# Attention a's outputs: halves and transposes moved from the tail into the head slots

## The reference

```python
x = x + _L0_attn_a_ref(_layernorm(x), Wq, Wk, Wv, bq, bk, bv, Wo, bo)   # 16 heads, softmax(q k^T / 8) v, then out @ Wo + bo
x = x + _L0_ffn_ref(_layernorm(x), w1, b1, w2, b2)                      # relu(x w1 + b1) w2 + b2, width 512
x = x + _L0_attn_b_ref(_layernorm(x), W_qk, W_v, alibi_slope)           # causal, scores + (kpos - qpos) * slope
x = x + _L0_ffn_ref(_layernorm(x), w1, b1, w2, b2)
return x
```

## Time and profile before

| | us |
|---|---|
| three runs | 563.72, 560.90, 563.49 |
| median | 563.49 |
| span of the profiled execution | 561.3 |
| PE busy | 526.3 (94%) |
| DVE busy | 446.3 (80%) |
| ACT busy | 469.0 (84%) |
| POOL busy | 453.8 (81%) |

### The profile page before, as it was taken

How to read it: one execution, slowest core, us unless ns; L and a number is a source line. 1 busy time by engine, 2 the same in 40 slices (tenths; PEclk the granted TensorE clock), 3 DMA queues, 4 the chain that set the end, 5 groups by cost and what they waited for, 6 DMA issues and landing times.

```text
span 561.3 us, 17932 instructions
## 1 busy us (share of the span) xinstructions
PE 526.3 (94%) x6864; PEld 371.1 (66%) x6864; DVE 446.3 (80%) x1382; ACT 469.0 (84%) x925; POOL 453.8 (81%) x447
## 2 busy tenths in 40 slices
PE   4888999999999999999999999998989998798897
PEld 3654666666666666766667666675679695656576
DVE  5878888888888888888888888887785575788943
ACT  3888998999988999989999899998973978573995
POOL 5678989888888888888888888888983977654885
PEclk9979999999999999999999999999999999998999
DMA  9442343332433324333243332435147100000002
GB/s 227 109 113 57 72 110 86 96 96 68 114 87 97 95 64 118 87 95 96 60 122 80 102 97 58 124 78 198 40 151 272 68 3 2 1 1 2 1 21 57
DMA packets 35461, 48.03 MB, mean 86 GB/s; under 512 B 10777, under 2 KB 16817, under 8 KB 35377
## 3 DMA queue, kind: packets, MB, share of 16 engines
q1 hardware_dynamic: 33264, 46.35, 30.2%
q10 hardware_dynamic: 2112, 0.54, 0.4%
HBM read 12.27 MB, written 9.44 MB: 39 GB/s over the span
## 4 chain that ended last, share of the span: by engine, by line
PE 75%; DVE 8%; issue 6%; ACT 5%; POOL 5%; DMA 1%; DVEq 0%; POOLq 0%; ACTq 0%
PE psum L562 11%; PE psum L620 10%; PE psum L621 10%; PE psum L516 7%; PE psum L518 6%; PE psum L517 6%; PE psum L600 6%; PE psum L602 6%; PE psum L601 6%; PE psum L623 2%; POOL h_lo L2146 1%; PE psum L781 1%; POOL rstd L2024 1%; ACT xn L1164 1%; DVE st_lo L1515 1%
## 5 line engine op out<-in xcount | busy, mean ns | idle before, releaser
L2079 POOL TENSOR_TENSOR p_hl<-p,p_hl 128x512 f16<-128x512 f32 x288 | 328.5, 1165 | 48.4 <-ACT p_hl L1264 44.6
L1532 DVE CUSTOM_DVE_ANT_0 max_junk<-psum,mask_s 128x1024 bf16<-128x1024 f32 (+7 forms) x256 | 190.4, 753 | 32.7 <-issue 32.6
L1263 ACT ACTIVATE p<-psum 128x512 f32<-128x512 f32 x288 | 175.9, 611 | 13.8 <-PE psum L623 12.2
L1264 ACT ACTIVATE p_hl<-psum 128x512 f16<-128x512 f32 x288 | 177.2, 615 | 0.0
L620 PE MATMUL psum<-q_hl,k_hh 128*128 128x512 f16 (+3 forms) x384 | 125.6, 327 | 0.5 <-ACT p_hl L1264 0.4
L600 PE MATMUL psum<-v_all,p_hl 128*128 128x65 f16 x1152 | 124.8, 193 | 1.1 <-POOL p_hl L2079 1.0
L601 PE MATMUL psum<-v_all,p_hl 128*128 128x64 f16 x1152 | 124.9, 192 | 0.0
L602 PE MATMUL psum<-v_all,p_hl 128*128 128x65 f16 x1152 | 124.4, 194 | 0.0
L621 PE MATMUL psum<-q_hm,k_l 128*128 128x512 f16 (+3 forms) x384 | 122.3, 327 | 0.0
L600 PEld LDWEIGHTS psum<-v_all,p_hl 128*128 128x128 f16 x1152 | 107.1, 98 | 16.1 <-POOL p_hl L2079 1.2
L601 PEld LDWEIGHTS psum<-v_all,p_hl 128*128 128x128 f16 x1152 | 106.2, 97 | 4.8
(11 more groups left out here) (206 smaller groups left out, 1109.1 us busy)
## 6 DMA issues: line engine op xcount, KB each, us to landing
k_hh<-st_hi SPq DMA_DIRECT2D x64, 128.0 KB, 2.3
o_scratch<-o_sb SPq DMA_DIRECT2D x16, 512.0 KB, 2.6
o_in<-o_scratch SPq DMA_DIRECT2D x8, 1024.0 KB, 8.6
q_hl<-st_hi SPq DMA_DIRECT2D x32, 128.0 KB, 2.4
q_hl<-st_lo SPq DMA_DIRECT2D x32, 128.0 KB, 2.4
k_l<-st_lo SPq DMA_DIRECT2D x32, 128.0 KB, 2.3
q_hm<-st_hi SPq DMA_DIRECT2D x32, 128.0 KB, 2.4
x_sb<-in_L_attn_a_x SPq DMA_DIRECT2D x4, 256.0 KB, 3.9
```

The source lines that it names most:

```text
L1263: nc.scalar.activation(p32[:, ring_at(u, r), :], src, ACT.Exp, scale=SCALE_A).then_inc(exp_done, 1)
L1264: nc.scalar.activation(p_hl[:, u % 2, 0, BANK * r:BANK * (r + 1)], src, ACT.Exp, scale=SCALE_A).then_inc(phi_done, 1)
L1532: nc.vector.tensor_tensor_reduce(out=max_junk[:, n % 2, 0:cols], in0=max_banks(v, j, 0, cols), in1=mask_s[:, S - cols:S], scale=1.0, scala ...
L2079: nc.gpsimd.tensor_tensor(p_hl[:, u % 2, 1, cols], p32[:, ring_at(u, r), :], p_hl[:, u % 2, 0, cols], ALU.subtract)\
```

## The change

The transposes of attention a's output no longer run on PE in the tail.

1. In slot u (from 2 on) ACT makes the high half of head u-2's output from `o_sb` (`output_high`, between the exponentials of unit 1 and unit 2), and DVE the low half (`output_low`, between the third maximum and the second projection piece). The inputs of `output_low` are `o_sb` and the high half, both in SBUF. `o_sb` has one buffer in place of two.
2. In every odd slot from 3 on SP issues two DMA transposes of f16 from SBUF to SBUF for a pair of heads (`turn_pair`), and in the next even slot the store of the turned pair (`store_pair`). `output_high` of the next pair waits for the transposes, since it overwrites their source.
3. `load_outputs` loads turned halves straight into the matmul's layout; chunk 0 in slot 28, chunk 1 in slot 30, chunks 2 and 3 (7 blocks of 8) after the last scores. The last pair is transposed by four DMAs straight into place.
4. `turn_block`, `block_high` and `block_low` are gone. `output_tile` of chunks 0 and 1 runs in PE's last slot; of chunks 2 and 3 the first 7 blocks (`output_first`) run ahead of the last one (`output_last`).
5. `tail_high` and `tail_low` move into slots 12 to 17, one each per slot. `add_output_row` moves from POOL to DVE, two at the end of slot 30 and two after it.
6. The lists of the tail are written anew in another order on PE, ACT, DVE and POOL.

The core of the diff:

```diff
-    HIGH_AT = {(HEADS - 3, 1): 0, (HEADS - 3, 2): 1, (HEADS - 2, 0): 2, (HEADS - 2, 1): 3, (HEADS - 2, 2): 4}
+    HIGH_AT = {12: 0, 13: 1, 14: 2, 15: 3, 16: 4, 17: 5}
...
+            def turn_pair(pair):
+                sp.wait_ge(o_lo_done, 2 * pair + 2)
+                if pair:
+                    sp.wait_ge(scratch_out, 16 * pair)
+                for half in range(2):
+                    sp.dma_start_transpose(o_turn[:, half, :].rearrange("f (t p) -> f t p", p=P), o_hl[:, half, :, :].rearrange("p t f -> p (t f)"))\
+                        .then_inc(o_turned, 16)
...
+                if u % 2 == 1 and u >= 3:
+                    turn_pair((u - 3) // 2)
+                if u % 2 == 0 and u >= 4:
+                    store_pair((u - 4) // 2)
...
+            def output_high(w):
+                act.wait_ge(o_ready, NG * (w + 1))
+                if w % 2 == 0 and 0 < w < HEADS - 2:
+                    act.wait_ge(o_turned, 32 * (w // 2))
+                cols = slice(DH * (w % 2), DH * (w % 2) + DH)
+                nc.scalar.copy(output_halves(w)[:, 0, :, cols], o_sb[:, :, cols]).then_inc(o_hi_done, 1)
...
+            def output_low(w):
+                dve.wait_ge(o_hi_done, w + 1)
+                cols = slice(DH * (w % 2), DH * (w % 2) + DH)
+                halves = output_halves(w)
+                nc.vector.tensor_tensor(halves[:, 1, :, cols], o_sb[:, :, cols], halves[:, 0, :, cols], ALU.subtract).then_inc(o_lo_done, 1)
...
                 maximum(2)
+                if u >= 2:
+                    output_low(u - 2)
                 project(1)
...
                 outputs(1)
                 tail_weights(2)
+                if u in HIGH_AT:
+                    tail_low(HIGH_AT[u])
+                if u == HEADS - 2:
+                    add_output_row(0)
+                    add_output_row(1)
...
-            for n in range(6):
-                tail_low(n)
-            def block_low(c, blk):
...
-                for j in range(CT):
-                    last = nc.tensor.transpose(bank(TR_BANKS[n % 3])[:, P * j:P * (j + 1)], o_in[c % 2][:, blk, j, :], ident[:, :])
-                last.then_inc(ot_full, 1)
```

More of the change, by code:

```diff
@@ L294, in hybrid_block @@
         small_in, late_in = sem("small_in"), sem("late_in")
-        o_back = [[sem(f"o_back{c}_{half}") for half in range(2)] for c in range(2)]
-        scratch_out = [sem("scratch_out0"), sem("scratch_out1")]
+        o_back = [sem(f"o_back{c}") for c in range(CHUNKS)]
+        o_hi_done, o_lo_done, o_turned, o_ended = sem("o_hi_done"), sem("o_lo_done"), sem("o_turned"), sem("o_ended")
+        scratch_out = sem("scratch_out")
         result_out = sem("result_out")
@@ L391, in unit_heads, with output_halves @@
             return slice(GH * g, GH * (g + 1)), m // (GH * GROUPS), 2 * (m % GH)
+        def output_halves(w):
+            return o_hl if w < HEADS - 2 else o_last
         def units_for(w):
@@ L784, in result_free @@
             def result_free(k, j):
-                if k == 0:
+                stage, c = K_ORDER[k]
+                if c == 0 and stage == 0:
+                    pe.wait_ge(max_done, QT * HEADS)
+                elif c == 0 and stage == 1:
                     pe.wait_ge(phi_done, NU * HEADS)
                 else:
-                    pe.wait_ge(res_done, 2 * (k - 1) + j // 2 + 1)
+                    before = k_of[stage, c - 1] if c else k - 1
+                    pe.wait_ge(res_done, 2 * before + j // 2 + 1)
@@ L791, in output_tile, with output_blocks @@
+            def output_blocks(c, j, blocks, starts=True, stops=True):
+                rows, cols = slice(P * j, P * (j + 1)), slice(P * (j % 2), P * (j % 2) + P)
+                for blk in blocks:
+                    last = three(bank(Y_BANKS[0][j // 2])[:, cols], oT[c][:, 0, blk, rows], oT[c][:, 1, blk, rows], wo_hi[:, blk, :], wo_lo[:, blk, :],
+                                 start=(blk == 0 and starts), stop=(blk == OB - 1 and stops))
+                return last
             def output_tile(c, j):
@@ L793, in output_tile @@
                 if j == 0:
-                    pe.wait_ge(ot_lo_done, OB * (c + 1))
+                    pe.wait_ge(o_back[c], 32)
                     pe.wait_ge(wts_lo_done, 2)
                 result_free(k_of[0, c], j)
-                rows, cols = slice(P * j, P * (j + 1)), slice(P * (j % 2), P * (j % 2) + P)
-                for blk in range(OB):
-                    last = three(bank(Y_BANKS[0][j // 2])[:, cols], oT_hi[:, c % 2, blk, rows], oT_lo[:, c % 2, blk, rows], wo_hi[:, blk, :], wo_lo[:, blk, :],
-                                 start=(blk == 0), stop=(blk == OB - 1))
@@ L801, in output_tile, with output_first, output_last @@
-                last.then_inc(y_full, 1)
+                output_blocks(c, j, range(OB)).then_inc(y_full, 1)
+            def output_first(c, j):
+                if j == 0:
+                    pe.wait_ge(o_back[c], 32)
+                result_free(k_of[0, c], j)
+                output_blocks(c, j, range(OB - 1), starts=(j % 2 == 0))
+            def output_last(c, j):
+                pe.wait_ge(o_ended, 64)
+                output_blocks(c, j, range(OB - 1, OB), stops=(j % 2 == 1)).then_inc(y_full, 1)
@@ L949, in outputs_b @@
                         last.then_inc(pvb_done, 1)
[L952 to L954 removed]
+            outputs(HEADS - 2, 0)
+            output_tile(0, 0)
+            output_tile(0, 1)
+            scores(HEADS - 1, 0)
+            scores(HEADS - 1, 1)
+            output_tile(0, 2)
+            output_tile(0, 3)
+            scores(HEADS - 1, 2)
+            scores(HEADS - 1, 3)
+            scores(HEADS - 1, 4)
+            output_tile(1, 0)
+            scores(HEADS - 1, 5)
+            output_tile(1, 1)
+            outputs(HEADS - 2, 1)
+            outputs(HEADS - 2, 2)
+            scores(HEADS - 1, 6)
+            scores(HEADS - 1, 7)
+            scores(HEADS - 1, 8)
+            outputs(HEADS - 2, 3)
+            outputs(HEADS - 2, 4)
+            outputs(HEADS - 2, 5)
+            outputs(HEADS - 2, 6)
+            outputs(HEADS - 2, 7)
+            outputs(HEADS - 2, 8)
             outputs(HEADS - 1, 0)
[L956 removed]
             outputs(HEADS - 1, 1)
[L958 to L960 removed]
+            output_tile(1, 2)
+            output_tile(1, 3)
+            turn_late(ln_of[1, 0])
             outputs(HEADS - 1, 2)
[L962 removed]
             outputs(HEADS - 1, 3)
             outputs(HEADS - 1, 4)
[L965 to L966 removed]
             outputs(HEADS - 1, 5)
@@ L1291, in act_slot @@
                 exponentials(u, 1)
-                tail_weights(0)
+                if u == HEADS - 3:
+                    tail_weights()
+                if u >= 2:
+                    output_high(u - 2)
                 exponentials(u, 2)
```

528 lines of the change are left out of this document (209 added, 319 removed).

## The result

The changed kernel takes 569.91 us (median of four runs, 569.82 to 573.79) where the kernel before, on the same chip, takes 563.24 us (four runs, 560.90 to 563.72). The ratio is 1.0146 with a 95% interval of 1.011 to 1.018: 1.5% slower. The forecast was 576 us in a range of 560 to 608.

A forecast was written before the change was run, and what follows sets the result against it. PE was taken as the bound, with DVE also on the path in the slots. +18.9 + 8.6 + 1.0 - 16.0 = +12.5 us, put onto the median of 563.5 us, gave 576 us; range 560 to 608 us.

The forecast's parts named there:

- 1, `output_low`: In the slots, DVE's `output_low` ahead of `st_lo`, on the path: 29 x 0.65 = 18.9 us, with DVE likelier ahead of POOL.
- 2, cast: In the slots, ACT's extra cast, 0.48 to 0.6 us: covered by DVE's `output_low`; without that cover 0.5 us.
- 3, weights in slots 12 to 17: DVE's `tail_low` on the path there: four at 1.57 us and two at 1.17, 8.6 us; 3 us if POOL is free.
- 4, DMA: In the slots, two transposes per pair have a window of some 9 us; cost nothing.
- 5, bias rows: End of slot 30, two additions on DVE, 0.66 to 1.25 us each; about 1 us on the path.
- 6, tail: PE loses 17.6 us of transposes; 1.5 us less idle, 3 us of new waits: gain of 16 us, bounds 9 and 22.
- rival A: DVE comes behind POOL in every slot: 45.5 us in place of 18.9, 603 us; chance 0.27 with mixtures.
- Rival B: Tail from 401 us on: new order also closes PE's waits, gaining more than slots cost; 560 or 555 us; chance 0.14.
- Rival C: Transposes outlast their window, ACT waits in each even slot, 14 times: 115 us in all, 690 us; chance 0.09.

## Why the prediction came out as it did

**Direction and size.** 576 us were forecast, 569.9 measured; slower as said. The sum had +12.5 us on the span, and the span grew by 6.7. Step by step:

| step | forecast | measured |
|---|---|---|
| 1, `output_low` | 18.9 | 16.6 (0.56 a slot, 0.90 in slot 29) |
| 2, cast | 0, covered | 0, covered (0.51 if alone) |
| 3, weights in slots 12 to 17 | 8.6 | 7.7 |
| 4, DMA | 0 | 0 |
| 5, bias rows | 1.0 | 0 in the slots; they run at 426.8 us, in the tail |
| first slot | not named | -0.6 (it differs by more from trace to trace) |
| 6, tail | -16 | -17.2 |

**Step 1** is right in place, mechanism and nearly in price. The cost is read exactly: `st_lo` later by 0.56 us, slot longer by 0.56 us. 0.66 was the distance in the earlier trace rows between two starts (0.65 in the sum), and the text called it a floor; here it is 0.60 (308.98 - 308.38), and the cost is another 0.04 us lower. Before, `st_lo` started 0.04 us behind the end of its input on ACT (313.90, 313.94) and 0.92 us behind the third maximum; now DVE goes on 0.88 us behind it. The call between 0.66 and 1.57 us was made from when POOL's third instruction would start, put at up to 0.15 us behind DVE: measured 0.08. The kernel with the cast left out turned it round by an estimated 0.14 us and paid 0.9 us a slot. In slots 29 and 30, which have no projection and whose timing the forecast didn't look at, rival A did come about, and slot 29 paid 0.34 us more for it. So the forecast was right here by an argument that had a margin of a tenth of a microsecond; nothing in the text could have put rival A much below its 0.27.

**Step 3** came near by two errors that cancel. The four subtractions of 512 columns took 0.85 us each and not 1.57 (their slots grew by 1.1, one by 1.4), the two of 128 columns 1.27 us each with slots longer by 1.5, where 1.17 was put. The second error is a term that the forecast lacked: in just these six slots `output_low` takes 1.07 to 1.40 us in place of 0.69. The kernel with cast and subtraction left out separates the two. Its six slots grow by 4.8 us together, which is the weights; the other 2.9 of the 7.7 us come with the cast and the subtraction.

```profile
L1597 DVE SCALAR_TENSOR_TENSOR w_lo<-w_raw,tail_gains,w_hi 128x512 f16<-128x512 f32 x2 | 1.7, 855 | 0.0
L1597 DVE SCALAR_TENSOR_TENSOR wo_lo<-wo_raw,tail_gains,wo_hi 128x512 f16<-128x512 f32 x2 | 1.7, 852 | 0.0
L1597 DVE SCALAR_TENSOR_TENSOR wqk_lo<-wqk_raw,tail_gains,wqk_hi 128x128 f16<-128x128 f32 x1 | 1.3, 1276 | 0.0
```

These are groups of instructions with busy time and mean ns. A subtraction of 128 columns takes longer here than one of 512: the price of this kind is set more by where POOL stands than by its size.

**Step 6** had the right total, in part by luck: PE's work in the tail fell by 16.3 us and its idle time by 1.1. But the text took it for granted that work which goes is time. In the order of before it was not: three quarters of the work left out gave 6.5 us in the profiled tails, and 4.1 us between medians. The rest of the 17.2 us came with the other parts of the rewrite (order, loads, the weights' subtractions), and which of them gave it is not shown. Rival B said that the new order would close the idle time of the second half as well. It didn't: behind 461 us PE idles for 5.2 and 10.8 us in the changed kernel, where it had idled for 15.0. What the order closed lies ahead of that, 0.9 us against 8.5 in the kernel with the work left out and the old order.

**Rival C** fell with room to spare in the time (5 us for the two) and less in the window (7.0 us where 9 were put, since SP reaches the transposes later: its moves of k are issued 0.59 us each, and they wait for the later `st_lo`). The page VectorE: DVE Perf Modes of the Trainium skill, section The three transpose paths, would have given an estimated 21 us for the sixteen blocks; the trace shows about 5. The page Advanced Engine Details and Errata of the Trainium skill, section X-Bar Transpose (TRN2), which has them as fast as plain DMAs, is nearer, but not met either: a plain store of 512 KB lands in 3.3 us here, one transpose of half that size in 3.9.

**What stays open**: which part of the rewrite closed the tail's idle time ahead of 461 us, and why the granted clock of the version with the weights moved reached 0.997 in one run and 0.985 in two others, which makes its range of 1.2% (others stay within 0.3 to 0.8%).

## What to carry to other kernels

Before an instruction is put into a loop on an engine with 20% idle time, find where in the loop that idle time lies: the same two instructions cost 16 us ahead of the value that PE waits for and, placed behind it, nothing in an undisturbed slot. The last turns of a loop can fall out another way than the middle ones, so read those too. Where two engines exclude each other, price an instruction by who starts first there, draw both engines' start times after every edit, and remember that an edit on a third engine moves one of them. And when work is taken from the bound, ask what lay in the waits that it had filled: here, in the old order, about half of it stayed as idle time.

## What the runs showed of the hardware

- A subtraction on DVE with two SBUF inputs and one on POOL exclude each other by order of start, and a lead of less than a tenth of a microsecond can decide. DVE first by 0.08 us: DVE 0.69 us, POOL 1.62 in place of 1.16. POOL first: DVE 1.67 us at a lead of 0.04 us, 1.61 at 0.10, 1.47 to 1.48 at 0.23, 1.37 at 0.34 and 1.26 at 0.45, and the addition of the earlier trace rows 1.33 at 0.38 us. In all of these DVE takes 1.71 us less the lead, within 0.01; it ends 0.55 us behind the point where POOL's usual 1.16 us would end. So the dearest start is the one just behind POOL's. Leaving out 0.5 us of ACT's work in each slot turned the order round and made the kernel 15 us slower (585.34 for 569.91).
- A DMA transpose from SBUF to SBUF of 128x1024 elements of f16 holds its queue for 1.35 us and lands 3.9 us after its issue (median of 30); the four smaller ones of the last pair land in 2.5 us.
- The granted clock of the tail's first stretch was 1.00 in the changed kernel with PE busy for 35.06 of 35.99 us, and 0.86 with the products thinned and PE busy for 29.81 of 36.30 us, with 3 us at 0.50 just behind an idle stretch of 4.1 us. No run holds the work fixed and changes the clock, and busy time alone does not sort the kernels: with both parts left out of the old order the clock there was 0.97 with PE busy for 50.57 of 59.11 us, and with the transposes alone left out 0.91 with 52.20 of 59.39 us.
